# Two adjacency buffers moved by 32 bytes: a graph layer in split float32r on one core

## What is computed

```python
def _cxin_conv(x, a, eps, W, b):
    ax = a @ x                       # (4096 x 4096) @ (4096 x 128)
    h = ax + (1.0 + eps[0]) * ax
    for i in range(3):
        h = relu(h @ W[i].T + b[i])  # 128 x 128 weights
    return h
h = jnp.maximum(_layernorm(x, axis=-1), 0.0)
out1 = _cxin_conv(h,  adj, eps1, W1, b1)
out2 = _cxin_conv(x2, adj, eps2, W2, b2)
x + concatenate((out1, out2), axis=1) @ Wm.T + bm
```

## Time and profile before

| | us |
|---|---|
| median of 3 runs | 406.56 (406.36 to 406.57) |
| the profiled execution | 406.39 |
| its span, from the first to the last instruction | 404.7 |
| TensorE busy, matmul | 400.2 (99%) |
| TensorE busy, weight load | 325.4 (80%) |
| VectorE busy | 219.1 (54%) |
| ScalarE busy | 219.4 (54%) |
| GpSimd busy | 30.5 (8%) |

### The profile page before, as it was taken

The page is one execution under the profiler, slowest core; times in us unless marked ns, Lnnn a source line. Parts: engine busy times, 40 slices in busy tenths (PEclk is TensorE's granted clock), DMA queues, the critical chain, the costliest instruction groups (busy, mean ns, idle before and its releaser), DMA issues.

```text
span 404.7 us, 4822 instructions
## 1 busy us (share of the span) xinstructions
PE 400.2 (99%) x1751; PEld 325.4 (80%) x1751; DVE 219.1 (54%) x258; ACT 219.4 (54%) x259; POOL 30.5 (8%) x35
## 2 busy tenths in 40 slices
PE   8999999999999999999999999999999999999997
PEld 2788888888888888888888888888888888888886
DVE  3998887656464434551645517345373444755223
ACT  4877667657564533555433556334565335766034
POOL 0243332100010000000100001000000000000100
DMA  7997786754636165334574336653175550740100
GB/s 303 420 377 285 296 314 238 244 208 160 232 146 210 44 241 205 109 120 191 186 280 164 122 128 236 230 206 141 67 262 204 207 196 38 275 166 2 52 0 28
DMA packets 14029, 76.21 MB, mean 188 GB/s; under 512 B 1920, under 2 KB 2176, under 8 KB 6080
## 3 DMA queue, kind: packets, MB, share of 16 engines
q1 hardware_dynamic: 12240, 71.18, 46.9%
q0 software_dynamic: 1200, 3.93, 2.9%
q10 hardware_dynamic: 576, 0.92, 0.6%
HBM read 73.93 MB, written 2.10 MB: 188 GB/s over the span
## 4 chain that ended last, share of the span: by engine, by line
PE 97%; DMA 2%; ACTq 0%; DVE 0%; issue 0%; DVEq 0%
PE acc L591 24%; PE acc L588 24%; PE acc L587 24%; PE second_acc L587 3%; PE second_acc L591 3%; PE second_acc L588 3%; PE hidden L588 3%; PE hidden L591 3%; PE hidden L587 3%; PE acc L605 2%; PE second_acc L605 2%; DMA adj_raw<-adj_first 2%; PE second_acc L619 1%; PE merged L588 1%; PE merged L591 1%; PE merged L587 1%
## 5 line engine op out<-in xcount | busy, mean ns | idle before, releaser
L588 PE MATMUL acc<-adj_hi,feat_hi 128*128 128x512 f32 x432 | 168.1, 389 | 0.0
L587 PE MATMUL acc<-adj_hi,feat_lo 128*128 128x512 f32 x432 | 168.1, 389 | 0.0
L591 PE MATMUL acc<-adj_lo,feat_hi 128*128 128x512 f32 x432 | 168.0, 389 | 0.0
L447 DVE TENSOR_TENSOR adj_lo<-adj_raw,adj_hi 128x2048 fp32r<-128x2048 f32 x48 | 108.3, 2289 | 36.7 <-ACT adj_hi L277 35.8
L277 ACT ACTIVATE adj_hi<-adj_raw 128x2048 fp32r<-128x2048 f32 x48 | 90.3, 1925 | 16.5 <-PE acc L591 14.6
L453 DVE TENSOR_TENSOR act_lo<-act_f,act_hi 128x512 fp32r<-128x512 f32 x60 | 41.0, 690 | 105.3 <-ACT act_f L297 105.3
L588 PEld LDWEIGHTS acc<-adj_hi,feat_hi 128*128 128x128 f32 x432 | 81.1, 188 | 17.1
L587 PEld LDWEIGHTS acc<-adj_hi,feat_lo 128*128 128x128 f32 x432 | 81.1, 188 | 17.1
L591 PEld LDWEIGHTS acc<-adj_lo,feat_hi 128*128 128x128 f32 x432 | 81.1, 188 | 16.8
L296 ACT ACTIVATE act_hi<-hidden,bias 128x512 fp32r<-128x512 f32 x45 | 30.9, 687 | 96.2 <-PE hidden L591 96.2
L507 DVE TENSOR_TENSOR adj_lo<-adj_raw,adj_hi 128x2048 fp32r<-128x2048 f32 x14 | 31.5, 2289 | 6.5 <-ACT adj_hi L315 6.2
(11 more groups left out here) (91 smaller groups left out, 251.3 us busy)
## 6 DMA issues: line engine op xcount, KB each, us to landing
adj_raw<-adj_tiles SPq DMA_DIRECT2D x62, 1024.0 KB, 5.1
x_rows<-x_tiles SPq DMA_DIRECT2D x15, 256.0 KB, 7.1
x_res<-x_t POOLq DMA_DIRECT2D x8, 256.0 KB, 6.4
out_t<-y_sb POOLq DMA_DIRECT2D x7, 256.0 KB, 2.3
adj_raw<-adj_second SPq DMA_DIRECT2D x2, 512.0 KB, 6.6
adj_raw<-adj_first ACTq DMA_DIRECT2D x2, 256.0 KB, 5.0
adj_raw<-adj_first SPq DMA_DIRECT2D x2, 256.0 KB, 4.7
w_raw<-w_t SPq DMA_DIRECT2D x1, 512.0 KB, 5.8
```

Source lines behind the costliest of these rows:

```text
L447: nc.vector.tensor_tensor(adj_lo[:, u % RING, :], adj_raw[:, u % RING, :], f32(adj_hi[:, u % RING, :]), ALU.subtract).then_inc(lo_made, 1)
L587: nc.tensor.matmul(out, lhs_lo, rhs_hi, start=start, stop=False)
L588: nc.tensor.matmul(out, lhs_hi, rhs_hi, start=False, stop=False)
L591: return nc.tensor.matmul(out, lhs_hi, rhs_lo, start=False, stop=stop)
```

## The change

Two unused buffers are declared, one of 8 float32 (32 bytes) ahead of `adj_hi` and one of 24 float32 (96 bytes) behind `adj_lo`.

```diff
+    LINE, SHIFT = 32, 8
...
         adj_raw = sb("adj_raw", [P, RING, UNIT_COLS])
+
+        sb("before_adj", [P, SHIFT])
         adj_hi = sb("adj_hi", [P, RING, UNIT_COLS], F32R)
         adj_lo = sb("adj_lo", [P, RING, UNIT_COLS], F32R)
 
+        sb("before_features", [P, LINE - SHIFT])
         feat_hi = sb("feat_hi", [P, 2, BLOCKS, D], F32R)
```

## The result

The changed kernel takes 417.62 us (median of 4 runs, 417.57 to 417.67) against 406.46 us in the same series: ratio 1.0275, 95% interval 1.0257 to 1.0292. That is 11.2 us more, where 10.6 us were forecast.

What follows compares the result with a forecast made beforehand. The prediction took TensorE's distance between matmul starts as the bound: 406.56 us plus 10.6 us (1,512 matmuls at 7 ns), all other parts at 0, gives 417.2 us; the 8-in-10 range is 402.0 to 421.7 us.

Steps and rivals of the forecast that it cites:

- What bounds the kernel: TensorE, busy 400.2 of 404.7 us; the quantity that counts is the distance between matmul starts, 226.5 ns in aggregation.
- VectorE, ScalarE at 0: Subtraction and rounding on the shifted adj_hi and adj_lo were costed at 0, with large cover from TensorE.
- The count, 1,512 matmuls, and 7 ns each: Float32r adjacency matmuls of the aggregation: 1,512, each 7 ns longer from start to start, 10.6 us in all.
- Whether a stream that is shifted uniformly settles: Open question whether aggregation matmuls, all shifted alike, return to 226.5 ns spacing; not settling was taken as likelier.
- the loose regime: TensorE matmul starts 230 to 235 ns apart instead of 226.5; expected for all aggregation, chance 0.56, 412.5 to 421.7 us.
- act_hi and act_lo begin at 96: Layer matmuls whose moving operands start off a 128-byte line run 7 ns longer on average; taken as model for shifted adjacency.
- buffers moved by whole lines; 0: Transfers to buffers shifted by whole 128-byte lines, and weight loads of the moved feat_hi and feat_lo, were taken at 0.
- the disputed term: TensorE's moving operand, adj_hi and adj_lo, at 32 modulo 128: 10.6 us more, bounds 6.0 and 15.1 us.
- longer weight loads (188 ns): Sign in the changed profile: if TensorE's weight loads grew from 188 ns, the features' move by a line is the cause.
- the prediction's own theory: The place of TensorE's moving operand within its 128-byte line sets the distance between matmul starts.
- No change: Rival: layer stretches come from switching between buffer places, so a uniformly shifted aggregation settles at 226.5 ns; 406.6 us, chance 0.22.
- Faster: Rival: weight load and moving stream, 32 bytes apart, stop colliding in aggregation; up to 15.1 us less, 391.4 us, chance 0.22.

Runs made afterwards that it cites:

- f1_both: Against the kernel before: adj_hi, adj_lo, feat_hi and feat_lo all begin at 32 modulo 128; 407.23 us, ratio 1.0025.
- f2_features_only: Against the kernel before: only feat_hi and feat_lo begin at 32 modulo 128, adjacency stays at 0; 416.10 us, ratio 1.0241.
- h1: Against the kernel before: weights and activations begin at 0 modulo 256, adjacency and features stay at 128; 405.71 us, ratio 0.9984.
- f4_line_only: Against the kernel before: adjacency stays, features and all buffers behind them move by one whole line of 128 bytes; 415.26 us, ratio 1.0218.

## Why the prediction was right in its number and wrong in its cause

**What bounds the kernel.** Right: only the distance between TensorE's starts counts. In all fourteen kernels TensorE stays busy for 99% of the span.

**VectorE, ScalarE at 0.** Right: 2,288 and 1,929 ns against 2,289 and 1,925.

**The count, 1,512 matmuls, and 7 ns each.** Right in size: 7.4 ns, 11.2 us, but by luck, as the next paragraphs show. The forecast range of 4 to 10 ns holds all kernels at 32 to 128 bytes.

**"Whether a stream that is shifted uniformly settles".** The choice for the loose regime was right for the change: not one of its 1,512 distances is below 229 ns. But the reason given, "act_hi and act_lo begin at 96", that is the place of the moving operand in a line, is the step that failed. f1_both shifts the stream as the change does and settles; f2_features_only does not shift it and stays loose. What the layers showed in the earlier trace rows was, as far as the runs separate it, for the greater part a distance: act_hi less w_hi is 213,600 - 201,152 = 12,448 bytes, 160 modulo 256, which puts w_hi 96 bytes beyond act_hi. The change has its features 96 bytes beyond the adjacency modulo 256 (256 - 160): the same distance. The prediction saw that "in both the moving operand is 32 bytes further on than the stationary one within its line", and used it only as a likeness, with a line of 128. So the 7 ns were read off matmuls that happen to lie as the changed ones do, for a reason that does not hold, and that 10.6 us came so near 11.2 us is luck. A part of those 7 ns belongs to the seams and not to the distance inside the layer: with that distance at 0 the three means were still 391, 389 and 393 ns in h1.

**"buffers moved by whole lines; 0".** Wrong, and nearly by as much as the disputed term: f4_line_only, which does nothing else, costs 9.0 us. The forecast sign for it, longer weight loads (188 ns), does not serve either: the mean of the adjacency's loads lies between 187.1 and 188.9 ns in all fourteen kernels, fast and slow, and only the matmuls draw apart. Two errors that hid each other: had the change moved adjacency and features together, the prediction's own theory would have given 417 us, and 407.2 would have come out.

**The rivals.** "No change" rested on a stream that is shifted uniformly settling again; that mechanism exists (f1_both), but needs the stationary operand shifted too. "Faster", on moving stream and weight load passing each other once they are apart, is the opposite of what runs: at distance 0 they go best, and the 13 ns above the columns are there at distance 0 in all kernels. (The weight load of the earlier trace rows starts 3 or 4 ns behind its matmul; the 10 ns of the prediction are the rounding of the timeline.) The formula of the Trainium skill, "TensorE: Matmul & The Clock Gate", section "Back-to-back issue gap", would give all fourteen kernels one distance. The section calls it the gap of an isolated matmul and gives some 131 ns for 512 columns in a stream of weight loads and matmuls, also without an address. Neither agrees with this case: here the same columns at the same granted clock of 1.00 take 226.7, 234.5 or 237.1 ns by address alone.

## What to carry to other kernels

In a kernel like this one, whose TensorE streams 512-column float32r matmuls without a gap, lay out everything that it moves and loads so that all buffers begin at one place modulo 256 bytes, small tables and activations too. A helper buffer or an odd-sized one declared in between cost 1.5 to 4% here, and putting it right costs some unused bytes. Other column counts and data types were not run. Look for it in the means of matmuls of equal shape: if they differ between buffers (389 here, 393 to 399 there) with nothing waited for, addresses are a suspect. And a control that is meant to leave something unmoved (here "the same place in a line of 128") deserves a run of its own.

## What was not expected of the hardware

- The period is 256 bytes: 128 bytes of distance cost 9.0 us, 256 and 512 nothing.
- The distance from start to start has a tight form (226.7 ns for 512 columns) and loose ones (single distances of mostly 229 to 241 ns), and a disturbance of either kind, a standstill or a few matmuls with operands elsewhere, can be followed by up to ten loose matmuls even where all operands lie well. It need not be: behind the layers of both branches in the kernel before there is none.
- Four bytes of distance cost more (237.1 ns) than 32 to 128 bytes (232.9 to 234.5 ns).
- VectorE (2,288 to 2,290 ns for a unit), ScalarE (1,923 to 1,930 ns) and the weight loads (187 to 189 ns) show none of it, at any place tried.
